# GpSimd's subtraction for the second direction's x row waits for a later row to be rounded by VectorE (two-layer ConvLSTM, one core)

## The reference

```python
def step(carry, xr):                       # one row: xr (B, C, W)
    h, c = carry
    inp = concatenate([xr, h], axis=1)     # 96 channels
    gates = conv1d(inp, w_mid, 'SAME') + b # 4*48 channels, 3 taps along W
    i, f, g, o = split(gates, 4, axis=1)
    c2 = sigmoid(f) * c + sigmoid(i) * tanh(g)
    h2 = sigmoid(o) * tanh(c2)
    return (h2, c2), h2
hs_f = scan(step, rows 0..63)              # direction 0
hs_b = scan(step, rows 63..0)              # direction 1
y = w_proj @ concatenate([hs_f, hs_b]); y = batch_norm(y); return relu(y) + x
```

## Time and profile before

| what | value |
|---|---|
| median of 3 runs | 1986.39 us (1983.12 to 1989.28) |
| profiled execution, its own time | 1985.13 us |
| its span, first to last instruction | 1983.2 us |
| mean granted TensorE clock | 0.93 of full speed |
| recurrence of L1 | about 281 to 805 us of the span |
| recurrence of L2 | from about 921 us on, to the same pattern |
| `split_hi` (L809) in the loops, median | 722 ns |
| `split_lo` (L693), median | 1201 ns |
| load of an x row into `xf`, issue to landing, median | 2.2 us |

### The profile page before, as it was taken

The page is one execution under the profiler, slowest core; times in us unless marked ns, Lnnn a source line. Parts: engine busy times, 40 slices in busy tenths (PEclk is TensorE's granted clock), DMA queues, the critical chain, the costliest instruction groups (busy, mean ns, idle before and its releaser), DMA issues. The chain is left out here.

```text
span 1983.2 us, 41167 instructions
## 1 busy us (share of the span) xinstructions
PE 1589.4 (80%) x13002; PEld 935.5 (47%) x13002; DVE 1475.4 (74%) x2699; ACT 1172.0 (59%) x2257; POOL 642.3 (32%) x577
## 2 busy tenths in 40 slices
PE   8979248888888888704888888888860899999997
PEld 6535125555555555203555555555520344445444
DVE  4539978888888888646888888888856766666666
ACT  1116128888888888543888888888853344444431
POOL 2010035555555555203555555555500000000000
PEclk9989669999999999857999999999985799999999
DMA  3769366666666666666666666667576011011100
GB/s 108 254 196 211 97 137 108 108 106 107 107 107 107 107 106 91 113 147 131 106 107 107 107 107 107 107 108 108 81 121 164 14 34 34 21 31 35 35 19 25
DMA packets 132266, 199.40 MB, mean 101 GB/s; under 512 B 28528, under 2 KB 47824, under 8 KB 131920
## 3 DMA queue, kind: packets, MB, share of 16 engines
q1 hardware_dynamic: 132176, 198.08, 53.7%
HBM read 73.72 MB, written 37.75 MB: 56 GB/s over the span
## 5 line engine op out<-in xcount | busy, mean ns | idle before, releaser
L720 PE MATMUL gates_l<-xh_l,w_l 128*112 128x512 f32 x3072 | 801.5, 409 | 122.3 <-ACT xh_l L757 122.1
L720 PEld LDWEIGHTS gates_l<-xh_l,w_l 128*112 128x112 f32 x3072 | 500.3, 175 | 422.8 <-issue 288.8
L684 POOL TENSOR_TENSOR xh_l<-hs,xh_l 48x512 fp32r<-48x512 f32 x252 | 300.5, 1192 | 442.0 <-ACT xh_l L757 442.0
L693 POOL TENSOR_TENSOR xh_l<-xf_l,xs_l 48x512 fp32r<-48x512 f32 x256 | 311.7, 1217 | 33.2 <-DVE xs_l L809 32.8
L720 PE MATMUL gates_l<-xc_l,w_l 128*112 128x512 f32 x512 | 164.6, 403 | 135.1 <-DVE begun_l L829 135.1
L853 DVE TENSOR_TENSOR hs<-gate_o_l,tanh_c_l 48x256 f32 (+1 forms) x512 | 193.3, 416 | 73.9 <-ACT tanh_c_l L786 70.1
L1292 PE MATMUL b_dw<-b_hid,b_diag 32*32 32x512 f32 x6840 | 235.3, 602 | 0.0
L786 ACT ACTIVATE tanh_c_l<-cell_l 48x256 f32<-48x256 f32 x512 | 158.1, 342 | 91.4 <-DVE cell_l L844 91.4
L776 ACT ACTIVATE gate_if_l<-gates_l 112x512 f32<-112x512 f32 x256 | 151.4, 591 | 99.8 <-PE gates_l L720 96.6
L844 DVE TENSOR_TENSOR cell_l<-keep_l,gates_l 48x512 f32<-48x512 f32 x256 | 178.5, 697 | 26.7
L840 DVE TENSOR_TENSOR gates_l<-gate_if_l,gates_l 48x512 f32<-48x512 f32 x256 | 178.4, 697 | 21.5
(11 more groups left out here) (150 smaller groups left out, 1436.3 us busy)
## 6 DMA issues: line engine op xcount, KB each, us to landing
xc_l<-xs_l SPq DMA_DIRECT2D x512, 99.0 KB, 3.0
xh_l<-xs_l SPq DMA_DIRECT2D x512, 66.0 KB, 2.4
xf_l<-rows SPq DMA_DIRECT2D x256, 96.0 KB, 2.2
hs<-rows SPq DMA_DIRECT2D x32, 384.0 KB, 10.3
rows<-hs SPq DMA_DIRECT2D x32, 384.0 KB, 5.1
xr<-in_x_rows SPq DMA_DIRECT2D x24, 256.0 KB, 2.7
xc<-in_x_cols SPq DMA_DIRECT2D x24, 256.0 KB, 3.0
mixed<-stage SPq DMA_DIRECT2D x24, 256.0 KB, 3.0
```

What stands on the lines that cost most here:

```text
L684: pool.tensor_tensor(inner(xh[n:n + C, d, 1 - s, LO, :]), whole, inner(xh[n:n + C, d, 1 - s, HI, :]).bitcast(F32), ALU.subtract).then_inc( ...
L693: pool.tensor_tensor(inner(xh[f:f + C, d, s, HI, :]), wide(xf[f:f + C, s, :]), inner(x_rows(s, slice(f, f + C))).bitcast(F32), ALU.subtrac ...
L720: return nc.tensor.matmul(ps[d][m][0:K, :], w[:, d, q, m, :], padded(tile)[:, :, lo:lo + W], start=first, stop=last)
```

## The change

`split_lo` gets an argument `rounded`, the value of `x_hi` to wait for. For direction 0 it stays t+1 in the function's own counting, which is the row that it reads. For direction 1 it is now one more: 2k+s+4, with the row behind it rounded too, or H = 64 at most, since no more rows are there. As the limit of 64 is reached in the step pair k = 30, that pair is written out, and POOL's loop runs 30 times instead of 31. No arithmetic changes, and on the other engines no instruction.

```diff
-                def split_lo(t, d, s):
+                def split_lo(t, d, s, rounded=None):
 
                     f = far[d]
-                    pool.wait_ge(x_hi, t + 1)
+                    pool.wait_ge(x_hi, t + 1 if rounded is None else rounded)
...
+                def rows_rounded(k, s):
+
+                    return min(2 * k + (s + 4), H) if isinstance(k, int) else 2 * k + (s + 4)
+
                 def step(k, last=False):
                     for s in range(2):
                         for d in range(2):
                             if not last:
-                                split_lo(2 * k + (s + 2), d, s)
+                                split_lo(2 * k + (s + 2), d, s, rows_rounded(k, s) if d == 1 else None)
                             if not last or s == 0:
                                 state_lo(2 * k + s, 2 * k + s if d == 0 else k * -2 + (H - 1 - s), d, s)
-                with pool.Fori(0, H // 2 - 1) as k:
+                with pool.Fori(0, H // 2 - 2) as k:
                     step(k)
+                step(H // 2 - 2)
                 step(H // 2 - 1, last=True)
```

## The result

The changed kernel takes 1972.79 us in the median (1969.42 to 1974.73) against 1986.02 us for the kernel before in the same comparison: ratio 0.9927, with a 95% interval of 0.9909 to 0.9944 (the ratios here and below are formed over all runs, and so differ a little from those of the medians). The forecast was 1990.1 us: the change makes the kernel faster, and I had no change or a small loss as the likeliest. What the recurrences gained can be read from the traces apart from the rest of the kernel: their length went from 521.50 and 521.52 us to 516.74 and 516.81, 9.5 us in all.

What follows compares the result with a forecast made beforehand. VectorE's own chain was taken to bound direction 1's half-step: 0.43 + 0.18 + 1.20 + 0.15 + 0.03 = 1.99 us against 1.96. Over 122 steps that adds 3.7 us to 1986.39, giving 1990.1 us, range 1972 to 2000.

Steps and rivals of the forecast that it cites:

- What bounds the kernel, and why the rounding of x took 0.72 us: Direction 1's half-step: VectorE's own chain sets the time; its x rounding waits for POOL's subtraction, 0.72 us instead of 0.43.
- The rounding of h takes the block over: Direction 1: VectorE's rounding of h, asked for at 705.88, finds POOL busy to 706.39 and ends 0.15 us later.
- rival 3: Rounding of h runs its full 0.29 us after POOL: 0.17 us a step slower, 2007 us; chance 0.07.
- POOL gets the count 0.18 us after the rounding's end: Direction 1's subtraction on POOL starts 0.18 us after VectorE's x rounding ends; bounds 0.15 and 0.27.
- The other terms of the sum: Rounding of x 0.43 us, POOL's subtraction 1.20, what is left of the rounding of h 0.15, next multiplication 0.03 later.
- main case: The summed chain in direction 1's half: 0.00 to +0.07 us a step, 1986 to 1995 us; chance 0.65.
- h starts at 0.52 after the cell: Direction 1: VectorE's start on h, bound by ACT's tanh, comes 0.52 us after the cell's end, a gain of 0.26.
- SP's queue, `state_lo` and the written-out pair: Next-row load 1.38 us later, SP keeping 2 us slack; `state_lo` not late; writing out the pair costs nothing, 1 us at worst.
- rival 2: Rounding of h held up for less than POOL's recorded 1.20 us; 0.05 to 0.2 us less gives 1966 to 1984; chance 0.15.

Runs made afterwards that it cites:

- e3: Changed kernel with direction 1's subtraction in the loops left out, a one-column subtraction counting in its place: 1969.12 us, ratio 0.9917 to the kernel before.
- e1: Changed kernel with POOL's wait on the x rounding carried by a register instruction ahead of direction 1's subtraction: 1985.10 us, ratio 0.9998 to the kernel before.
- e6: As e4, but the second half placed ahead of direction 0's subtraction, right behind `state_lo` of direction 1: 1964.85 us, ratio 0.9911 to the kernel before.
- e5: The changed kernel timed once more, word for word: 1971.92 us against 1982.70 for the kernel before, ratio 0.9951.
- e4: Changed kernel with direction 1's subtraction in two 256-column halves, the second in the next step behind direction 0's subtraction: 1995.05 us, ratio 1.0052 to the kernel before.

## Why the prediction was wrong

- *What bounds the kernel, and why the rounding of x took 0.72 us:* right. Alone it takes 0.43 in every step.
- *The rounding of h takes the block over:* right, and shown by e3. That it ends 0.15 us after POOL was right too (0.16 in the steps shown of the changed kernel and of e1, 0.15 in the median), and with it rival 3, full length after the end of POOL's record, is out. The word of the Trainium skill (SBUF — State Buffer, Who interferes with whom) that the other fully blocks fits the wait. Why less than the full length is left after POOL's record isn't shown. The prediction has the start-up of the blocked instruction lie in the wait. But if POOL gave the ports back about 0.14 us before its record ends, and the blocked instruction then ran in full, it would end at the same moment: 0.29 - 0.15 = 0.14 us for the rounding of h, 0.43 - 0.29 = 0.14 for that of x. Both readings also leave the roundings of e6 alone. They give the same time for this change.
- *POOL gets the count 0.18 us after the rounding's end:* this is the step that failed, by its size. I took it from the earlier trace rows as "the row with the same two instructions", and that was wrong on what the listing of POOL's order ahead of the prediction showed: the row is the subtraction of direction 0 in a loop's first step, whose wait on `x_hi` is carried by a register instruction (`L692 REGISTER_ALU [waits a_x_in0]`), while that of direction 1 carries this wait itself. It measured 0.08, below my lower bound of 0.15 too, which came from PE's wait for ACT. e1 put a register instruction there and got 0.16, the forecast's period (8.18 against 8.21) and no change of the time. 0.10 us too much in each of 122 steps is 12 us. In all the forecast of 1990.1 us was 17.3 above the measured 1972.79: 13.2 of that in the recurrences (+3.7 forecast, -9.5 measured), and 4.1 outside them, where e5 and e1 show no gain.
- *The other terms of the sum* held: 0.43, 0.15 and 0.03 as taken, and 1.19 for POOL instead of 1.20. The chain came out at 1.88 us instead of 1.99, by the handoff and this 0.01. The forecast's price of the change, +3.7 us, was the small difference of two sums of near 2 us, so an error of 5% in one of them decided the sign. I had the main case "good to 0.01 or 0.02 us" for each term, which the bounds that I wrote beside the handoff (0.15 to 0.27) contradict.
- *h starts at 0.52 after the cell:* wrong, it was 0.63 (707.21 to 707.84), with no wait for ACT's tanh and 0.17 us of issue behind the rounding. From there to the rounding of h were 0.88 us, not the 0.81 that I took from direction 0's half. So that rounding was asked for 1.48 us after the start of the rounding of x, not 1.30, and took 0.37 to 0.38 instead of 0.66. POOL hid both, since the rounding of h ends with it.
- *SP's queue, `state_lo` and the written-out pair:* right, nobody waits for them. In e4 the SP load became late, when the release of `xf` moved by a further 3.4 us (POOL ends 5.15 us after the start of the x rounding there, 1.70 in the changed kernel): the forecast had counted SP's slack for the queue, not for a later release.
- *Rivals:* the time fell into what I had given rival 2, faster by a part of the 0.26 us, but by another mechanism: the block ended where the forecast had it, 0.15 us behind POOL, and POOL had started early. That 1972.79 lies inside the range, whose lower end of 1972 was set by rival 2, is luck.

## What to carry to other kernels

When two blocking instructions stand in each other's way, moving one moves the block to the next instruction of the kind; price the chain start to end, and if the difference is a few hundredths of a us, where the wait stands (on the instruction, or on a register instruction before it) belongs in the sum. Cut the blocker in pieces that fit the holes, as in e6, and follow whom the last piece releases: in e4 the same pieces in another order made the recurrences 29.9 us longer than in e6, by a DMA that started later.

## What the runs showed of the hardware

- A wait that stands on POOL's own instruction let it start 0.08 us after VectorE's end, and behind a register instruction that carries the wait 0.16 us (e1, both in one profile). The first subtraction ahead of L1 in the kernel before started at 266.80, 0.19 us after its rounding (266.19, 0.42 us long); its wait on `x_hi` stands on an instruction ahead of it that only waits, so it goes with the slower kind.
- A subtraction of 256 columns on POOL took 0.69 us, one of 512 took 1.19 (e6), so half the columns cost 58% of the time.
- A VectorE instruction that was blocked by POOL ended 0.15 to 0.16 us after it with 256 columns (0.29 when free) and 0.29 with 512 (0.43 when free), so about 0.14 us less than its free length in both; whether it had begun while it waited, or POOL let go before its record's end, isn't shown. One that was asked for up to 0.11 us before POOL's end lost nothing (e6).
- The recurrences repeat to 0.2 us in two profiles of one kernel (1033.55 and 1033.39), while the rest of the span went from 933 to 945 us over the seven profiles of the changed kernel and those derived from it, and from 935 to 945 over 22 runs of the kernel before.
